# Probability products by whole quads, with the side jobs placed anew

## The chip, the cores and the metric

The kernel runs on one core of a Trainium2 chip. A core has five engines that run at once and meet only at semaphores: TensorE (PE, matmuls; its weight loads are shown as PEld), VectorE (DVE), ScalarE (ACT), GpSimd (POOL), and SyncE (SP), which here only issues DMAs. Matmul results go to PSUM, which has eight banks of 128 x 512 f32; all eight are in use. The metric is the time of one execution in microseconds (us), lower is better.

## The reference

Eight rows of 512 tokens and 256 features go through a cross attention with 16 heads of size 16, and then a linear two-layer network with its own weights for each row. All is f32.

```python
x = x + xattn(layernorm(x), ctx, ctx)          # per row b of 8:
#   q = (ln(x) @ Wq.T + bq) / 4 ; k = ctx @ Wk.T + bk ; v = ctx @ Wv.T + bv
#   attn = softmax(q k^T) for 16 heads ; y = x + (attn v) @ Wo.T + bo
h1 = einsum('gmh,goh->gmo', ln(y)[g], W1[g]) + b1[g]
h2 = einsum('gmo,gho->gmh', h1, W2[g]) + b2[g]  # no activation between
out = y + h2
```

Since nothing stands between the two layers, the kernel forms W1 and W2's product (w21) for each row and applies that.

## The kernel before

**Units.** The 16 heads of a row are four quads of four heads, and a quad has 16 units: four heads by four blocks of 128 keys. A row thus has 64 units, u = 0 to 63, and the program of every engine is one loop over rows (a turn) with an inner, unrolled loop over u. In a unit TensorE computes `st`, transposed scores of one head and key block (128 keys x 512 queries) of row b, and `nat`, the same scores the other way round (queries on partitions), 28 units ahead (LEAD), partly of row b+1. The two use different halves of the array's rows (64 x 128 tiles) and overlap. VectorE takes the row maximum of each `nat` (`neg_max`, L1036), ScalarE the exponential of each `st` into `probs` (L860). The maxima go into `st` as an additional row of the operand `qs`, so those of a quad must be there before its first `st`: they are turned by two small matmuls (`maxT`, L534, one for each half of the rows), copied to `max_hi` by VectorE (L1042), and carried to `qs` by a DMA (`store_max`, L367).

**Buffers.** `st` has 2 PSUM banks: `st` of unit u waits for the exponential of u-2. `nat` has 3, used as a ring, in which the turned maxima take a place too: a `nat` waits for the row maximum three places back.

**Probability products.** `pv(b, n)` (L547) multiplies the four exponentials of heads of one key block with V, in four 128 x 32 column tiles; four such calls, n = 4g to 4g+3, make a quad in the one bank `pv`. Before, two calls are made at u = 2, 10, 18, ... (L754), in what is called a bunch below, so a quad takes two bunches. Its result is copied out by ScalarE (`even_quad`, `odd_quad`), the sums of exponentials go through a DMA to `sums`, a reciprocal (`invert`, L1097) and two more DMAs (`save_inverse`, `spread_inverse`), and GpSimd multiplies (`divide`, L1305).

**Jobs.** Everything else of a row is cut into pieces, and tables give the unit after whose st and nat TensorE does each piece: XT (transposed normalised x, row b+1), K and Q (projections, row b+1, 12 pieces each), WO (output projection of row b-1, 8), V (row b+1, 8), YT (transposed normalised y, row b-1), Z (times w21, row b-1, 8), W21 (row b, 18, of which numbers 0 and 9 are the short ones of b2). All jobs share the two banks misc0 and misc1, so a job waits until the one before it has been copied out: K's result is copied by ScalarE and VectorE (`qk_move`) before Q may start, WO's is added to y and its statistics taken by VectorE (`y_half`, L1099, at the unit of WO's last piece and the next) before V may start, Z's is added to y (`out_half`, L1108) before W21 may start. `out_half` also waits for GpSimd's `add_b2`.

**Order.** Each engine works strictly in its written order; a wait holds up all that stands behind it. SP issues all DMAs of a turn in the order of its `turn` (L404), and GpSimd its work in that of L1340. The tables (L69 to L87) name units; EVEN, MASK, ODD, PAIR, INVERT, Y_NORM, CTX, X_STATS, X_NORM say where ScalarE and VectorE do their parts.

In the first turn there is no row before, so no WO, YT and Z; in the last none after, so no XT, K, Q and V, and no nat past u = 35.

## Time and profile before

| | |
|---|---|
| three runs, median (lowest to highest) | 552.11 us (547.64 to 553.07) |
| the profiled execution | 547.8 us, its span 545.9 us |
| mean granted TensorE clock | 0.994 |
| busy in the span: PE, DVE, ACT, POOL | 95%, 78%, 70%, 51% |

Times of rows are counted from the start of the span. A timeline row gives start, duration, engine, line, operation and tile; x8 means eight instructions merged, and one f32 matmul is two records. Durations of matmuls overlap, since they are pipelined, so what one costs is read from the distance of starts. What stands in brackets is the idle time ahead of it and what ended it.

### The profile page before, as it was taken

To read this page: it belongs to the slowest core of one execution; us is meant where nothing else is said; L and a number is where in the kernel's file an instruction comes from. 1 tells how busy PE (TensorE), PEld (TensorE's weight loads), DVE (VectorE), ACT (ScalarE), POOL (GpSimd) and SP (SyncE) were. 2 spreads that over 40 slices of the span, in tenths; PEclk is the share of its full clock that TensorE was granted. 3 is DMA by queue.
4 is the path that set the end of the run, shared out by engine and by line. 5 is a ranking of instruction groups with operands and counts; after the bars stand their busy time and mean duration, and the time that the engine had idled before them with its cause. 6 is when DMAs were issued, how large, how long until landed. Compare 5 with 4: busy or idle time off the path is not lost.

```text
span 545.9 us, 13272 instructions
## 1 busy us (share of the span) xinstructions
PE 521.2 (95%) x4229; PEld 328.9 (60%) x4229; DVE 425.7 (78%) x805; ACT 383.7 (70%) x707; POOL 276.3 (51%) x314
## 2 busy tenths in 40 slices
PE   8889999999999999999999999999999999899997
PEld 5555545675656665666666666567556766355556
DVE  4898887988887987888978988889878987785114
ACT  5437778767876768768786778768787776767732
POOL 3854606647356636648366454648276460309121
PEclk9989999999999999999999999999999999998999
DMA  6771245542454245450565235461554225340301
GB/s 209 184 249 76 61 112 144 161 135 60 135 161 177 60 111 168 141 166 21 134 168 201 59 68 150 139 201 26 116 152 178 64 61 146 74 173 2 99 0 39
DMA packets 34367, 65.29 MB, mean 120 GB/s; under 512 B 9810, under 2 KB 11930, under 8 KB 32282
## 3 DMA queue, kind: packets, MB, share of 16 engines
q1 hardware_dynamic: 34330, 64.81, 41.0%
q8 instruction: 21, 0.34, 0.3%
q14 instruction: 16, 0.13, 0.1%
HBM read 34.65 MB, written 4.44 MB: 72 GB/s over the span
## 4 chain that ended last, share of the span: by engine, by line
PE 67%; POOL 14%; DVE 9%; issue 4%; ACT 3%; DMA 1%; SPq 0%; POOLq 0%; DVEq 0%; ACTq 0%
PE pv L558 16%; PE st L544 12%; PE misc L671 10%; PE nat L527 8%; PE misc L630 8%; PE misc L643 6%; POOL b_part L1334 5%; DVE neg_max L1036 5%; POOL b_part L1329 4%; POOL y L1322 3%; ACT probs L860 2%; DVE y L1102 2%; DVE stats L1047 1%; POOL rstd L1264 1%; PE nat L583 1%
## 5 line engine op out<-in xcount | busy, mean ns | idle before, releaser
L1036 DVE TENSOR_REDUCE neg_max<-nat 128x1 f32<-128x512 f32 x512 | 329.4, 679 | 65.2 <-PE nat L527 64.1
L860 ACT ACTIVATE probs<-st 128x512 f32<-128x512 f32 x505 | 289.4, 598 | 113.0 <-PE st L544 102.3
L527 PE MATMUL nat<-ks,qs 63*128 63x512 f32 x512 | 237.1, 486 | 3.9 <-DMA qs<-lo 2.1
L544 PE MATMUL st<-qs,ks 64*128 64x512 f32 x505 | 231.0, 480 | 5.7 <-ACT probs L860 4.4
L544 PEld LDWEIGHTS st<-qs,ks 64*128 64x128 f32 x505 | 91.1, 186 | 75.3 <-ACT probs L860 44.4
L558 PE MATMUL pv<-probs,vs 128*32 128x512 f32 x1024 | 124.9, 605 | 0.0
L527 PEld LDWEIGHTS nat<-ks,qs 63*128 63x128 f32 x512 | 92.2, 185 | 19.5 <-DVE neg_max L1036 12.2
L671 PE MATMUL misc<-w_in 64*128 64x256 f32 x512 | 73.6, 378 | 0.0
L1261 POOL TENSOR_SCALAR var_eps<-mean_var 128x4 f32<-128x4 f32 x14 | 3.2, 227 | 119.5 <-DVE mean_var L1053 119.4
L558 PEld LDWEIGHTS pv<-probs,vs 128*32 128x32 f32 x1024 | 26.8, 109 | 56.6 <-issue 47.2
L671 PEld LDWEIGHTS misc<-w_in 64*128 64x128 f32 x512 | 50.6, 187 | 6.5 <-issue 0.8
L1315 POOL TENSOR_TENSOR y<-y,bo_all 128x256 f32<-128x256 f32 x32 | 22.4, 734 | 32.6 <-DMA y<-x 32.6
L1289 POOL TENSOR_TENSOR lo<-raw,hi 128x512 fp32r<-128x512 f32 x28 | 36.0, 1284 | 2.2
L1334 POOL TENSOR_TENSOR b_part<-b_part 128x1024 f32<-128x1024 f32 (+2 forms) x24 | 35.0, 1460 | 1.9
L1305 POOL TENSOR_TENSOR attnT<-pair_ctx,inv_sum 128x512 f32<-128x512 f32 x15 | 19.3, 1284 | 26.0 <-DMA inv_sum<-inv_dram 26.0
L643 PE MATMUL misc<-w,yT_in 64*128 64x256 f32 x224 | 31.0, 387 | 0.8 <-DVE yT_in L1069 0.2
L1287 POOL CAST hi<-raw 128x512 fp32r<-128x512 f32 x28 | 17.1, 611 | 28.6 <-DVE raw L1074 28.5
L643 PE MATMUL misc<-wo_in,attnT 64*128 64x256 f32 x224 | 31.3, 380 | 0.0
L1329 POOL TENSOR_TENSOR b_part<-w_in,b_in 128x2048 f32<-128x2048 f32 x8 | 28.8, 3603 | 0.0
L643 PEld LDWEIGHTS misc<-w,yT_in 64*128 64x128 f32 x224 | 22.2, 187 | 4.2 <-DVE yT_in L1069 3.0
L643 PEld LDWEIGHTS misc<-wo_in,attnT 64*128 64x128 f32 x224 | 22.4, 187 | 2.1
L1322 POOL TENSOR_TENSOR y<-y,b_all 128x256 f32<-128x256 f32 x28 | 19.5, 721 | 0.0
(155 smaller groups left out, 671.8 us busy)
## 6 DMA issues: line engine op xcount, KB each, us to landing
ks<-hi SPq DMA_DIRECT2D x64, 128.0 KB, 2.4
qs<-hi SPq DMA_DIRECT2D x64, 128.0 KB, 2.5
w_in<-w SPq DMA_DIRECT2D x8, 1024.0 KB
w_in<-w2T SPq DMA_DIRECT2D x8, 1024.0 KB
ctx_in<-ctxT SPq DMA_DIRECT2D x8, 512.0 KB, 4.7
ks<-lo SPq DMA_DIRECT2D x32, 128.0 KB, 2.4
qs<-lo SPq DMA_DIRECT2D x32, 128.0 KB, 2.5
y<-x SPq DMA_DIRECT2D x8, 512.0 KB, 3.4
```

Of the source, the lines that this page charges most:

```text
L527: mm(ring(at)[:, :], qs[rows, 2 * g + jj, c * P:(c + 1) * P], ks[rows, 2 * g + jj, :], start=True, stop=True).then_inc(nat_done, 1)
L544: mm(st_of(u, prep)[:, :], ks[rows, 2 * g + jj, kc * P:(kc + 1) * P], qs[rows, 2 * g + jj, :], start=True, stop=True).then_inc(st_done, 1)
L558: last = mm(pv_bank[32 * j:32 * j + 32, :], vs[:, kc, 4 * g + j, :], probs[n % 4][:, j, :], start=(kc == 0), stop=(kc == 3), tile_position ...
L630: last = mm(misc[m][:, :], (w_hi, w_lo)[left][rows, w, f, m * P:(m + 1) * P], src[right][rows, f, :], start=(i == 0), stop=(i == 11))
L643: last = mm(misc[half][:, s * D:(s + 1) * D], lefts[left][rows, f, c * P:(c + 1) * P], rights[right](rows, f), start=(i == 0 and n == 0), ...
L671: last = mm(misc[f][:, 0:D], w1_in[rows, o, f * P:(f + 1) * P], w2_in[rows, o, :], start=(phase == 0 and o == 0 and not b2), stop=(i == 2 ...
L860: act.activation(probs[kc % 4][:, j, :], st_of(u, prep)[:, :], ACT.Exp).then_inc(exp_done, 1)
L1036: dve.tensor_reduce(neg_max[:, g % 2, col:col + 1], ring(at_nat(n) if at is None else at)[:, :], AX.X, ALU.max, negate=True).then_inc(max_ ...
L1289: pool.tensor_tensor(lo[:, which, m, :], raw[:, which, m, :], hi[:, which, m, :].bitcast(F32), ALU.subtract).then_inc(lo_ready, 1)
L1322: last = pool.tensor_tensor(y[:, c, :], y[:, c, :], b2_all[:, :], ALU.add)
L1329: pool.tensor_tensor(b2_part[:, :, :], w2_in[:, :, :], b1_in[:, :].unsqueeze(2).to_broadcast([P, OC, D]), ALU.mult).then_inc(b2_step, 1)
L1334: pool.tensor_tensor(b2_part[:, 0:width, :], b2_part[:, 0:width, :], b2_part[:, width:2 * width, :], ALU.add).then_inc(b2_step, 1)
```

## The change

Two pv bunches of a quad become one bunch of four calls at u = 2, 18, 34, 50. `probs` grows from 16 to 19 tiles in a ring, so that three exponentials of the next quad can be written while a quad is still read. The maxima are turned one ring place later: the first half behind the unit's nat, the second behind its jobs, where they stood on both sides of st and nat. Nearly all tables change: K ends at 8 and Q begins at 10, WO ends at 25 and V begins at 28, Z ends at 49, and all of W21 is at 51 to 62. X's statistics go from 50 to 17, the copy of Q's other half from VectorE to ScalarE, the invert from 7 to 6, and the order of SP and GpSimd is changed.

```diff
-TURN_AFTER = 2
+AHEAD = 3
+TURN_AFTER = 3
-K_AT = (3, 4, 4, 4, 5, 5, 6, 7, 7, 8, 8, 9)
-Q_AT = (12, 12, 12, 12, 13, 13, 14, 15, 15, 16, 16, 16)
+K_AT = (3, 4, 4, 4, 5, 5, 6, 6, 7, 7, 8, 8)
+Q_AT = (10, 11, 12, 12, 12, 13, 14, 14, 15, 16, 16, 17)
...
-W21_AT = (44, 45, 46, 47, 48, 48, 52, 52, 54, 55, 56, 56, 57, 59, 60, 60, 61, 62)
+W21_AT = (51, 51, 52, 53, 54, 54, 55, 55, 56, 57, 57, 58, 58, 59, 60, 61, 61, 62)
...
+LAST_PV_AT = (56, 59, 62)
...
-        probs = [sb(f"probs{i}", [P, 4, S]) for i in range(4)]
+        probs = sb("probs", [P, 16 + AHEAD, S])
...
+        def prob_at(u):
+            g, i = u // 16, u % 16
+            return 16 - AHEAD + AHEAD * (g % 2) + i if i < AHEAD else i - AHEAD
...
                     turned = maxT_of(b, u, prep)
-                    if turned:
-                        maxT(*turned, TILES[1], prep).then_inc(maxT_half, 1)
                     st(b, u, prep)
                     for row, n in nats_of(b, u, post, prep):
                         nat(row, n)
                     if turned:
+                        maxT(*turned, TILES[1], prep).then_inc(maxT_half, 1)
+                    if u % 16 == 2:
+                        for n in range(4):
+                            if u > 16:
+                                pv(b, u // 16 * 4 - 4 + n)
+                            elif post:
+                                pv(b - 1, 12 + n)
+                    if not prep and u in LAST_PV_AT:
+                        pv(b, 12 + LAST_PV_AT.index(u))
+                    jobs(b, u, post, prep)
+                    if turned:
                         wait_apart(pe, maxT_half, 4 * turned[0] + turned[1])
                         maxT(*turned, TILES[0], prep).then_inc(maxT_done, 1)
-                    if u % 8 == 2:
-                        for n in (u // 4 - 2, u // 4 - 1):
...
-                if j == 0:
-                    wait(act, pv_done, 16 * b + kc - 3)
-                act.activation(probs[kc % 4][:, j, :], st_of(u, prep)[:, :], ACT.Exp).then_inc(exp_done, 1)
+                if u % 16 == AHEAD:
+                    wait(act, pv_done, 16 * b + u // 16 * 4)
+                act.activation(probs[:, prob_at(u), :], st_of(u, prep)[:, :], ACT.Exp).then_inc(exp_done, 1)
```

TensorE from the end of K to the start of Q (K's rows read ctx, Q's normedT), second turn, before:

```order
L630 MATMUL misc<-ctx_lo,w_hi 128x512 x2
L314 REGISTER_ALU
L544 MATMUL st<-qs,ks 128x512
L314 REGISTER_ALU
L527 MATMUL nat<-ks,qs 128x512
L558 MATMUL pv<-probs,vs 32x512 x8
...
L527 MATMUL nat<-ks,qs 128x512
L314 REGISTER_ALU
L630 MATMUL misc<-normedT_hi,w_hi 128x512 x2
```

and in the change:

```order
L638 MATMUL misc<-ctx_lo,w_hi 128x512 x2
L322 REGISTER_ALU
L552 MATMUL st<-qs,ks 128x512
L322 REGISTER_ALU
L535 MATMUL nat<-ks,qs 128x512
...
L535 MATMUL nat<-ks,qs 128x512
L322 REGISTER_ALU
L638 MATMUL misc<-normedT_hi,w_hi 128x512 x2
```

Between the two jobs stood three pairs of st and nat and a bunch; now two pairs stand there alone.

TensorE from the end of WO (it reads attnT) to the start of V (it reads ctx_hi with w_hi), same turn, before:

```order
L643 MATMUL misc<-wo_in,attnT 128x256 x4
L314 REGISTER_ALU
L544 MATMUL st<-qs,ks 128x512
...
L527 MATMUL nat<-ks,qs 128x512
L314 REGISTER_ALU
L558 MATMUL pv<-probs,vs 32x512 x8
...
L527 MATMUL nat<-ks,qs 128x512
L643 MATMUL misc<-w_hi,ctx_hi 128x256 x2
```

and in the change:

```order
L651 MATMUL misc<-wo_in,attnT 128x256 x4
L322 REGISTER_ALU
L552 MATMUL st<-qs,ks 128x512
...
L552 MATMUL st<-qs,ks 128x512
L322 REGISTER_ALU
L535 MATMUL nat<-ks,qs 128x512
L651 MATMUL misc<-w_hi,ctx_hi 128x256 x2
```

Three pairs stand in between in both, and the bunch has gone.

SP's DMAs from the gather of the sums to the spreading of their inverses (the load of ctx stood ahead of all this), now:

```order
L392 DMA sums<-even_sum 64x1x32
L393 DMA sums<-odd_sum 64x1x32
...
L350 DMA ctx_in<-ctxT 128x2x512
L322 REGISTER_ALU
L347 DMA x_in<-x 128x1024
...
L378 DMA qs<-max_hi 2x8x128
L322 REGISTER_ALU
L400 DMA inv_dram<-inv_small 4x16x32 x2
L322 ISA
L408 DMA inv_sum<-inv_dram 128x1x512
```

Here 1 MB of loads (ctx and x, 512 KB each) now stands directly ahead of the maxima and the inverses; only x stood there before, and the inverses were ahead of the maxima.

## Rows read from the trace of the kernel before

**Rows 1.** The page: busy time of each engine, share of the span, instructions.

```profile
PE 521.2 (95%) x4229; PEld 328.9 (60%) x4229; DVE 425.7 (78%) x805; ACT 383.7 (70%) x707; POOL 276.3 (51%) x314
```

**Rows 2.** Windows (length, busy by engine, clock, DMA share, GB/s): two whole turns.

```profile
280.59:343.50 62.91, 61.27 (x532) 39.44 (x536) 52.67 (x99) 47.02 (x89) 35.38 (x41) 1.00 0.43 127
466.86:528.54 61.68, 58.61 (x400) 30.33 (x404) 28.70 (x55) 40.80 (x77) 20.17 (x22) 0.97 0.22 71
```

**Rows 3.** Windows: one middle turn, from the bunch at u = 2, 18, 34, 50.

```profile
217.65:232.30 14.65, 14.65 (x116) 9.17 (x114) 12.61 (x22) 10.68 (x20) 9.08 (x11) 1.00 0.53 151
232.30:247.89 15.59, 15.46 (x147) 10.69 (x146) 13.38 (x29) 10.24 (x20) 7.25 (x10) 1.00 0.45 138
247.89:264.62 16.73, 15.89 (x143) 10.26 (x146) 14.05 (x24) 12.92 (x24) 10.12 (x9) 1.00 0.25 56
264.62:280.59 15.97, 15.32 (x134) 9.32 (x138) 12.72 (x27) 13.25 (x28) 8.53 (x13) 1.00 0.58 169
```

**Rows 4.** Timeline of PE around a bunch of two calls.

```profile
231.55 0.39 PE L544 MATMUL st<-qs,ks 64*128 64x512 f32 x1
...
231.81 0.49 PE L544 MATMUL st<-qs,ks 64*128 64x512 f32 x1
...
232.30 1.92 PE L558 MATMUL pv<-probs,vs 128*32 128x512 f32 x16
234.16 0.50 PE L544 MATMUL st<-qs,ks 64*128 64x512 f32 x1
...
234.50 0.39 PE L544 MATMUL st<-qs,ks 64*128 64x512 f32 x1
```

**Rows 5.** The chain that ended last (start, length, what): a single call.

```profile
528.54 0.99 PE pv L558 x8
```

**Rows 6.** Timeline of PE: two units with one W21 piece each.

```profile
262.03 0.58 PE L544 MATMUL st<-qs,ks 64*128 64x512 f32 x1
...
262.69 0.57 PE L544 MATMUL st<-qs,ks 64*128 64x512 f32 x1
```

**Rows 7.** Timeline of PE: the last matmuls of K.

```profile
224.41 0.43 PE L630 MATMUL misc<-ctx_lo,w_hi 64*128 64x512 f32 x2
```

**Rows 8.** Timeline of DVE: K's copy, and six reductions in a row.

```profile
225.53 0.73 DVE L1074 TENSOR_SCALAR raw<-misc,bqk 128x512 f32<-128x512 f32 x1
...
244.23 3.64 DVE L1036 TENSOR_REDUCE neg_max<-nat 128x1 f32<-128x512 f32 x6
```

**Rows 9.** Timeline of PE: last row of WO, first of V.

```profile
239.47 0.38 PE L643 MATMUL misc<-wo_in,attnT 64*128 64x256 f32 x1
...
242.70 0.39 PE L643 MATMUL misc<-w_hi,ctx_hi 64*128 64x256 f32 x2
```

**Rows 10.** Timeline of DVE: the two halves of WO's result.

```profile
239.89 0.69 DVE L1102 TENSOR_TENSOR y<-misc,y 128x512 f32<-128x512 f32 x1
...
241.97 0.68 DVE L1102 TENSOR_TENSOR y<-misc,y 128x512 f32<-128x512 f32 x1
```

**Rows 11.** Waits of DVE from 200.4 to 263.3 (us in total, times, longest).

```profile
DVE y L1111 <- POOL y L1322: 1.0, 1, 1.0
```

**Rows 12.** Timeline of SP's queue and of POOL: sums, inverses, divide.

```profile
221.28 0.56 SPq L385 DMA_DIRECT2D sums<-odd_sum  x1
...
224.69 1.14 SPq L392 DMA_DIRECT2D inv_dram<-inv_small  x2
...
227.21 0.62 SPq L400 DMA_DIRECT2D inv_sum<-inv_dram  x1
...
231.61 1.28 POOL L1305 TENSOR_TENSOR attnT<-pair_ctx,inv_sum 128x512 f32<-128x512 f32 x1 [1.09 <-DMA inv_sum<-inv_dram]
```

**Rows 13.** Windows: before and in a stretch with a lower clock, first turn.

```profile
32.60:38.00 5.40, 4.33 (x32) 2.50 (x30) 5.40 (x10) 2.78 (x5) 1.49 (x3) 1.00 0.93 277
38.00:41.40 3.40, 3.40 (x19) 3.13 (x16) 2.43 (x4) 1.19 (x2) 2.63 (x3) 0.50 0.98 391
```

**Rows 14.** The page, DMA issues: KB each, median us from issue to landing.

```profile
ctx_in<-ctxT SPq DMA_DIRECT2D x8, 512.0 KB, 4.7
```

105 lines of the change are left out of this document (49 added, 56 removed).

## The prediction

> **What bounds the kernel now.** I read the page first, then windows over whole turns and over the four quarters of a turn, then the timelines of TensorE and VectorE inside a turn, and last the waits. The page shows PE busy for 95% of the span, and DVE for 78% [rows 1]. The 95% overstates PE, since matmuls overlap in the records. A middle turn takes 62.9 us, of which DVE works 52.7 and ACT 47.0 [rows 2]; DVE has no more than 10 us of air in 63. PE and DVE are tied by a ring of three nat banks, so the slower of the two sets the pace of each short stretch: PE where jobs or bunches stand, DVE where units are bare. A bare pair of st and nat costs PE 0.26 us (231.55 to 231.81) [rows 4], a reduction costs DVE 0.61 (3.64 for six) [rows 8]. I take the turn in four quarters from bunch to bunch, which I call A (u = 2 to 18), B (18 to 34), C (34 to 50) and D (50 to 2): 14.65, 15.59, 16.73 and 15.97 us [rows 3], in sum 62.94.
>
> **What a bunch costs.** The pair ahead of it starts at 231.81 and the bunch at 232.30, so 0.49 where a pair takes 0.26: 0.23 to get in. From the bunch to the next pair it is 1.86 (232.30 to 234.16), and that pair takes 0.34 (to 234.50), 0.08 more than a pair [rows 4]. Two calls are 1.85 long [rows 4], one alone is 0.99 [rows 5], so a call more adds 0.86 and 0.13 is fixed. Entrance, fixed part and exit: 0.23 + 0.13 + 0.08 = 0.44, and up to 0.5 with the first weights. A bunch of four is 1.85 + 2 x 0.86 = 3.57. Four bunches fewer in a turn save 4 x 0.5 = 2.0 us, if PE is what everybody waits for at that place. This is the gain of the change, and it is sure only where nothing was hidden under the bunch.
>
> **What hid under the bunches that go.** Two of the four stood between two jobs on the same PSUM banks.
>
> K to Q (the bunch at u = 10, quarter A). K's last matmul starts at 224.41 [rows 7]; VectorE finishes its copy at 225.53 + 0.73 = 226.26 [rows 8], 1.85 later, since reductions stand ahead of it. Under the bunch nobody saw this. Now K ends at u = 8, Q starts at u = 10, and TensorE has only the rest of K (0.23) and two pairs (0.5) to do. It will stand at Q's first matmul for 1.85 - 0.73 = 1.1 us. Taking the pair copy out of the way (u = 3 to 12) makes VectorE's backlog 0.6 shorter at best, the earlier invert makes it 0.3 longer: 0.5 to 1.5, and I take 1.1. Behind the waiting matmul stand the next st and nat, so ACT and DVE run empty too. A then is 14.65, less the bunch at 10 (2.35 with its switch), plus two calls more in the bunch at 2 (1.71), plus 1.1, less 0.2 for the maxima (below): 14.9.
>
> WO to V (the bunch at u = 26, quarter B). WO's last matmul starts at 239.47, V's first at 242.70 [rows 9]: 3.2 us, set by VectorE, which adds the first half at 239.89, takes its statistics, does a reduction, and ends the second add at 241.97 + 0.68 = 242.65 [rows 10]. The bunch and three pairs filled all of that but 0.4. The change leaves three pairs, 0.8 us, so TensorE will stand for some 2.4 us ahead of V, with the nat banks full. V starts no sooner for the bunch having gone; its work is added at u = 18 instead. B is 15.59 + 1.71 (longer bunch) + 0.26 (one more pair ahead of WO's end) - 0.6 (V is done one unit sooner) - 0.2 = 16.8. If the wait were 1 us shorter, B were 15.8.
>
> C: the bunch at 42 goes (-2.35), that at 34 grows (+1.71), five W21 pieces and a short one move to D. A piece costs 0.66 (262.03 to 262.69) less a pair [rows 6], 0.42, the short one about half, in sum -2.35. The wait of `out_half` for GpSimd's `add_b2`, 1.0 us [rows 11], which held W21's start, should go too: `add_b2` now comes ahead of `b2_parts`, and Z ends under the long bunch at 50. Units 37 to 39 are bare now, and DVE's 0.61 sets their pace instead of PE's 0.26: 3 x 0.35, some 0.9. C is 16.73 - 2.35 + 1.71 - 2.35 - 1.0 - 0.2 + 0.9 = 13.4.
>
> D: the bunch at 58 goes, that at 50 grows, W21's pieces arrive: 15.97 - 2.35 + 1.71 + 2.35 - 0.3 = 17.4. The copy of W21 at u = 62 ahead of the next XT is as it was.
>
> **The turned maxima.** Now the first half no longer holds up st and nat, and the second is behind the jobs, so its wait for the first is filled. Nothing shows this price alone. Below it is nothing (DVE is late and the ring waits one place later anyway), above it is a pair and a half, 0.4, for each of four. I take 0.2 to 0.3.
>
> **Costs that I set at nothing.** The statistics of x (1.8 us of VectorE) go from the bunch at 50 to that at 18, which is 3.57 long and covers them with two reductions (1.2). Q's second copy on ScalarE falls under the same bunch. y's normalisation (2.1 us of ScalarE) falls under that at 34. Without that cover each would cost its own length once in a turn. The ring of 19 lets ScalarE go on for three units, but only two st banks feed it, so in a bunch of 3.57 it does two exponentials as before; this ring saves nothing by itself, it only makes the long bunch harmless.
>
> **Sum.** A 14.9 + B 16.8 + C 13.4 + D 17.4 = 62.5, against 62.94: 0.4 less, and times six turns 2.5 us. In the first turn the gain and the wait at Q nearly cancel, and W21 moves out of bare units, where it was free, into full ones: +1. The last turn, 61.68 long [rows 2], has no V and few jobs, so it is paced by ACT and DVE; it loses the cover of y's halves in B but is shorter in C: 0, give or take 3. From the profiled execution, 547.8, the sum is 547.8 - 2.5 + 1 = 546.3. A further low-clock stretch in the now longer runs of bare units (35 to 49 in the first turn, 3 to 17 in the last) would add 1.7, as 3.4 us at clock 0.50 cost [rows 13], and I count one: 548. The median of the runs shown, 552.1, is 4.3 above the profiled time; I put the forecast 1 above the sum on that account, 549.
>
> **Rivals.**
> Faster: the waits at Q and V come out small, because VectorE, which idles in each long bunch, arrives without backlog. For it speaks that DVE has 10 us of air in a turn [rows 2]. Against it speaks that both waits are chains of VectorE's own work behind PE's last matmul, 1.85 and 3.2 us long, and air elsewhere doesn't shorten them. Without either, DVE's work would bound A (14.1) and B (15.2): 0.8 + 1.6 = 2.4 us less in a turn, six turns, 14.4: 533 to 535. With half of it 541. Point of decision: waits below half of 1.1 and 2.4. Chance 0.31.
>
> Slower, by SP's order: the maxima and inverses, 8 KB each, now stand behind 1 MB of loads. Before, from the issue of the second sums at 221.28 to the end of GpSimd's division at 231.61 + 1.28 it took 11.6 us [rows 12]. That issue is 3.6 us behind the start of the bunch at 2 (217.65) [rows 3], and now 1.7 more: at 5.3, so the division ends at 16.9, and WO comes at 14.9 + 3.57 + 0.9 = 19.4, 2.5 us of slack. 512 KB of ctx take 4.7 us to land [rows 14]; I estimate both loads at 6 to 7, which is until 12.7. The inverses were on DRAM by 227.21, 5.9 behind the sums [rows 12], which would be 11.2 now: if they wait for the loads they are 1.5 late, and the slack shrinks to 1. The maxima would come at 12.7 too, and st of u = 16 wants them at some 13. If each small transfer loses 1 us more, either use is 1 to 2 us late, six times: 555 to 560. That is 0.14. The Trainium skill, DMA: Bandwidth & Descriptors, section on queues, rings and completion order, says that descriptors are consumed in ring order on each DMA engine, which would make small transfers of the same queue wait so; no row here shows a small one caught behind a large one.
>
> Slower, by the clock: in the first turn a stall of some 2 us after thin units was followed by 3.4 us at clock 0.50, which is 1.2 GHz of 2.4 [rows 13]. If the stall ahead of V does the same in each turn, V runs at half the clock and a turn gains 1.7 us: six times 1.7 is 10, 558. Against it: WO stands densely ahead of that stall, and the before kernel's stall ahead of XT never cost a clock in the middle turns (1.00) [rows 2]. Chance 0.13. The Trainium skill, TensorE: Matmul & The Clock Gate, Part 1, says the clock falls after the array has been idle and comes back with activity; by this rule a longer wait in every turn is a danger, and it speaks against this change.
>
> **How the numbers follow.** Forecast, within 1% (a measurement of this kernel can tell about 1%, 5.5 us, from no change): 0.42. Faster 0.31, slower 0.14 + 0.13 = 0.27. The range reaches from the half case of the faster rival with 3 us to spare, 538, to the clock rival with 2, 560; about 1 in 10 is left out at each end. The likeliest case's own range is 543 to 555 (quarters off by 0.5 us each way in six turns, first and last turn by 3).
>
> **What would show it.** In the profile after: bunches of 32 records 3.6 us long at u = 2, 18, 34, 50, four a turn. TensorE standing about 1.1 us ahead of the first Q matmul and 2.4 ahead of V's first, put down to VectorE. No wait of VectorE for GpSimd at `out_half`. Quarters near 14.9, 16.8, 13.4, 17.4 and a turn near 62.5. ACT's wait for st should be fewer and longer. I am wrong if V starts under 2.5 us behind WO's last matmul, if C doesn't shrink by 3 us, if PE waits for a DMA at u = 16 or 20, or if the clock falls in middle turns.

## The result and the profile after

The changed kernel takes 572.8 us in the median of its runs (569.9 to 576.4), the kernel before 552.6 beside it: a ratio of 1.040, 95% interval 1.035 to 1.046. That is slower by 4%, outside the range, on the side that had 0.27. The profiled execution has a span of 574.6 us, 28.7 more than before's 545.9. That is more than the 20.2 us between the medians: after's profiled execution is the slowest of its four (576.4 us, clock 0.950), before's is one of its fastest (547.8 us, clock 0.994), while other executions of before at 551.6 to 553.5 us have a mean clock of 0.978 to 0.984. The accounts below are of the two profiled executions.

In kernel.py of after, st is L552, nat L535, pv L566, K and Q L638, WO and V L651, the reductions L1044, the adds of WO's result L1110. The page of after, engines' busy time and the granted clock in 40 slices, beside [rows 1]:

```profile
PE 538.1 (94%) x4229; PEld 347.8 (61%) x4229; DVE 425.9 (74%) x798; ACT 386.1 (67%) x714; POOL 277.0 (48%) x314
PEclk9889879899999899998999899998999899887999
```

VectorE and ScalarE do the same work as before and idle more; the instructions of PE are the same in number. The clock's row is what is new: an 8 in nearly every turn. Its mean over the span is 0.950, before 0.994. At half clock for the rest, that is 0.050 x 2 x 574.6 = 57 us at 1.2 GHz against 7.

Windows of after over the quarters A, B, C and D of a middle turn, beside [rows 3] (length, busy by engine, clock, DMA share, GB/s):

```profile
230.46:245.50 15.04, 14.57 (x120) 9.34 (x118) 11.88 (x21) 10.37 (x20) 10.84 (x14) 1.00 0.62 183
245.50:263.88 18.38, 16.91 (x150) 11.95 (x148) 15.76 (x37) 11.17 (x20) 8.13 (x12) 0.91 0.41 118
263.88:277.94 14.06, 13.73 (x116) 8.64 (x112) 12.03 (x21) 11.89 (x23) 10.38 (x10) 1.00 0.34 111
277.94:295.26 17.32, 16.70 (x159) 12.11 (x156) 13.05 (x23) 13.75 (x28) 5.97 (x6) 1.00 0.30 88
```

The turn is 64.80 us instead of 62.94: A +0.4, B +2.8, C -2.7, D +1.35. B is the only quarter at a clock below 1.00. TensorE there, from WO's last matmul to V, beside [rows 9]:

```profile
254.88 0.38 PE L651 MATMUL misc<-wo_in,attnT 64*128 64x256 f32 x1
...
256.26 0.49 PE L535 MATMUL nat<-ks,qs 63*128 63x512 f32 x1
258.11 0.38 PE L651 MATMUL misc<-w_hi,ctx_hi 64*128 64x256 f32 x2 [1.35 <-DVE y L1110]
...
259.14 0.41 PE L651 MATMUL misc<-w_hi,ctx_hi 64*128 64x256 f32 x2
259.36 0.41 PE L651 MATMUL misc<-w_hi,ctx_lo 64*128 64x256 f32 x2
```

V starts 3.23 us behind WO's last matmul, to the hundredth what it was before (239.47 to 242.70); TensorE stands for 1.35 of them; the three pairs in between filled the rest, up to 256.26 + 0.49. Then V's rows come about 0.21 us apart. In a kernel below whose clock holds they are 0.12 apart. Waits of TensorE over the whole span (us in total, times, longest):

```profile
PE misc L651 <- DVE y L1110: 8.2, 6, 1.4
...
PE misc L638 <- POOL normedT_lo L1285: 4.8, 4, 2.0
```

The last of these is a wait of Q's first matmul, and 2.0 of it are in turn 1 (the second), as will be seen.

Spans of all turns, from the st of u = 2 to that of the next turn, us, by the windows of the traces. `early_y` and `fixed` are experiments told below:

| turn | 0 | 1 | 2 | 3 | 4 | 5 | 6 | 7 |
|---|---|---|---|---|---|---|---|---|
| before | 58.2 | 61.1 | 62.9 | 62.9 | 62.9 | 62.8 | 60.6 | 60.6 |
| after | 62.4 | 66.5 | 65.1 | 64.8 | 64.7 | 64.9 | 64.0 | 66.9 |
| early_y | 62.5 | 62.4 | 64.7 | 64.7 | 64.8 | 64.5 | 62.2 | 66.6 |
| fixed | 64.6 | 62.4 | 63.5 | 63.4 | 63.4 | 63.3 | 62.2 | 66.0 |

Of the 28.7 us, 1.5 are ahead of turn 0 (a low-clock stretch at 19.4), 8.1 in turns 2 to 5, 5.3 in turn 1, 3.4 in turn 6, and 10.5 in the first and last turn together. The stretch ahead of turn 0 comes and goes with the execution rather than with the change: `singles` and `best3` below, which begin as before does, have one at 19.6 and 17.7, and `early_y`, which begins as after does, has none.

### The profile page after: what moved, and what is told of

Read it like the earlier page. It is cut to its first block, busy times and chain, and to the rows that moved or that the text cites. A ratio compares the mean times of both kernels' runs of the same rounds, so it can differ in the third digit from the quotient of the medians.

```text
span 574.6 us, 13174 instructions
## 1 busy us (share of the span) xinstructions
PE 538.1 (94%) x4229; PEld 347.8 (61%) x4229; DVE 425.9 (74%) x798; ACT 386.1 (67%) x714; POOL 277.0 (48%) x314
## 4 chain that ended last, share of the span: by engine, by line
PE 66%; issue 11%; POOL 9%; DVE 7%; DMA 3%; ACT 3%; SPq 1%; DVEq 0%; POOLq 0%; ACTq 0%
PE pv L566 17%; PE misc L651 13%; PE st L552 11%; PE nat L535 8%; PE misc L638 5%; PE misc L679 5%; DVE neg_max L1044 4%; POOL normedT_lo L1285 2%; POOL y L1321 2%; ACT probs L867 2%; DVE y L1110 2%; POOL b_part L1340 2%; DMA inv_sum<-inv_dram 1%; POOL b_part L1335 1%; PE nat L591 1%
## 5 line engine op out<-in xcount | busy, mean ns | idle before, releaser
L1044 DVE TENSOR_REDUCE neg_max<-nat 128x1 f32<-128x512 f32 x512 | 332.9, 683 | 98.1 <-PE nat L535 95.6
L535 PE MATMUL nat<-ks,qs 63*128 63x512 f32 x512 | 256.9, 514 | 4.6 <-DVE neg_max L1044 2.2
L552 PE MATMUL st<-qs,ks 64*128 64x512 f32 x505 | 252.5, 510 | 6.3 <-ACT probs L867 4.2
L552 PEld LDWEIGHTS st<-qs,ks 64*128 64x128 f32 x505 | 97.6, 195 | 71.2 <-ACT probs L867 40.8
L566 PE MATMUL pv<-probs,vs 128*32 128x512 f32 x1024 | 122.0, 616 | 0.0
L535 PEld LDWEIGHTS nat<-ks,qs 63*128 63x128 f32 x512 | 98.8, 196 | 16.8 <-DVE neg_max L1044 10.6
L566 PEld LDWEIGHTS pv<-probs,vs 128*32 128x32 f32 x1024 | 30.4, 113 | 70.1 <-issue 58.5
L651 PE MATMUL misc<-w,yT_in 64*128 64x256 f32 x224 | 37.8, 379 | 0.0
L651 PE MATMUL misc<-wo_in,attnT 64*128 64x256 f32 x224 | 33.0, 379 | 0.0
L1302 POOL COPY vs<-v_nat 128x256 f32<-128x256 f32 x32 | 12.6, 398 | 35.4 <-DVE v_nat L1088 21.7
L651 PE MATMUL misc<-w_hi,ctx_hi 64*128 64x256 f32 x112 | 20.6, 357 | 8.2 <-DVE y L1110 8.2
L651 PEld LDWEIGHTS misc<-w,yT_in 64*128 64x128 f32 x224 | 27.0, 186 | 0.8 <-PE misc L651 0.2
L651 PEld LDWEIGHTS misc<-wo_in,attnT 64*128 64x128 f32 x224 | 23.3, 186 | 2.5
```

What stands on the lines that cost most here:

```text
L535: mm(ring(at)[:, :], qs[rows, 2 * g + jj, c * P:(c + 1) * P], ks[rows, 2 * g + jj, :], start=True, stop=True).then_inc(nat_done, 1)
L552: mm(st_of(u, prep)[:, :], ks[rows, 2 * g + jj, kc * P:(kc + 1) * P], qs[rows, 2 * g + jj, :], start=True, stop=True).then_inc(st_done, 1)
L566: last = mm(pv_bank[32 * j:32 * j + 32, :], vs[:, kc, 4 * g + j, :], probs[:, prob_at(4 * n + j), :], start=(kc == 0), stop=(kc == 3), til ...
L651: last = mm(misc[half][:, s * D:(s + 1) * D], lefts[left][rows, f, c * P:(c + 1) * P], rights[right](rows, f), start=(i == 0 and n == 0), ...
L1044: dve.tensor_reduce(neg_max[:, g % 2, col:col + 1], ring(at_nat(n) if at is None else at)[:, :], AX.X, ALU.max, negate=True).then_inc(max_ ...
```

## The experiments

Ratios are against the kernel before on the same chip, with 95% intervals. Quarters are of turn 3 unless another is named.

### The bunches by themselves

**bunch_only**: before, with one bunch of a quad, the ring of 19 and the last turn's three single calls (`LAST_PV_AT`), all tables of jobs and orders as they were.

```diff
-                    if u % 8 == 2:
-                        for n in (u // 4 - 2, u // 4 - 1):
+                    if u % 16 == 2:
+                        for n in range(4):
```

> The kernel before, with only the bunch changed: whole quads at u = 2, 18, 34, 50 and the ring of 19 tiles, every table, the maxima and the orders of SP and GpSimd as before. Theory 1 (bunches covered waits between jobs): four switches of 0.5 are saved in a turn, but the covers at u = 10 (K to Q), 26 (WO to V) and 42 (Z to W21) are gone; with V's stall of 2.3, Q's of 0.9, W21's wait for out_half of 1 to 2 us more, and a low clock behind the stall, a middle turn is 64 to 66 us and the whole 565 to 580. Theory 2 (the new tables and orders are at fault, the bunch is the gain): a middle turn is about 61, the whole 535 to 542.

Measured: 585.4 us, 1.066 (1.058 to 1.074), the slowest of the plain edits; theory 1, with the turn 0.7 and the whole 5 us above its ranges. Its quarters:

```profile
229.53:244.89 15.36, 14.79 (x123) 9.66 (x118) 12.41 (x22) 10.63 (x20) 9.13 (x10) 1.00 0.44 131
244.89:262.11 17.22, 15.37 (x148) 10.85 (x148) 13.37 (x28) 10.39 (x19) 7.45 (x10) 1.00 0.47 149
262.11:279.45 17.34, 16.14 (x142) 10.51 (x140) 14.30 (x24) 13.02 (x24) 10.62 (x9) 1.00 0.22 49
279.45:296.22 16.77, 15.11 (x134) 9.36 (x131) 12.45 (x27) 12.65 (x27) 7.66 (x12) 1.00 0.53 150
```

And the waits that its timeline of TensorE names in that turn, start first, wait and releaser in brackets (a sixth, 0.61 ahead of XT, is in before's turn as well, with 0.60):

```profile
240.33 0.50 PE L551 MATMUL st<-qs,ks 64*128 64x512 f32 x1 [0.49 <-ACT probs L866]
...
255.44 0.50 PE L551 MATMUL st<-qs,ks 64*128 64x512 f32 x1 [0.41 <-ACT probs L866]
257.42 0.39 PE L650 MATMUL misc<-w_hi,ctx_hi 64*128 64x256 f32 x2 [1.40 <-DVE y L1108]
...
275.78 0.49 PE L675 MATMUL misc<-b_part,ones 64*128 64x128 f32 x4 [0.93 <-DVE y L1117]
...
292.21 0.50 PE L551 MATMUL st<-qs,ks 64*128 64x512 f32 x1 [0.99 <-ACT probs L866]
```

The turn is 66.7 us with the clock at 1.00 throughout, 3.8 more than before, though it holds four switches fewer. TensorE's busy time is the same (14.79 + 15.37 + 16.14 + 15.11 = 61.4, before 61.3), so what is added is standing: the five waits are 4.2 us, of which before's turn has 0.74, at W21. A bunch that goes from between two jobs uncovers the wait for the copy of the first job's result (V's 1.40), and st runs into ScalarE three times, in A, B and D. That is 3.5 of the 3.8.

V waits 1.39 to 1.40 us in each of turns 1 to 6 of this kernel, but the clock falls only in 1, 2 and 5. B of turn 2, with the fall, to be read beside B of turn 3 above:

```profile
178.56:197.07 18.51, 16.66 (x150) 11.82 (x146) 14.13 (x29) 10.47 (x19) 9.02 (x10) 0.91 0.36 107
```

18.5 instead of 17.2, in one and the same execution: a stretch of 3.4 us at 0.50 costs 1.3.

**singles**: before, each bunch of two calls as two single ones, one unit apart; eight switches more in a turn.

```diff
-                    if u % 8 == 2:
-                        for n in (u // 4 - 2, u // 4 - 1):
+                    if u % 8 in (1, 2):
+                        n = u // 4 - 2 if u % 8 == 1 else u // 4 - 1
```

> The kernel before with each bunch of two calls parted into two bunches of one, a pair of st and nat between them (u = 1 and 2, 9 and 10, ...): the price of a switch by itself, with every wait between jobs covered as before. The prediction's price of 0.44 to 0.5 us gives eight switches a turn, 3.5 to 4 us: middle turn 66.4 to 66.9, the whole 549 + 7.5 x 4 = 576 to 580. If a switch costs nothing where TensorE is not the slowest (rival), under 65 and under 568.

Measured: 568.3 us, 1.033 (1.028 to 1.038). The turn is 65.1 us, 2.2 more for eight switches, 0.28 each:

```profile
229.55:244.53 14.98, 14.98 (x121) 9.12 (x117) 13.15 (x22) 11.42 (x20) 8.93 (x10) 1.00 0.51 154
244.53:260.31 15.78, 15.59 (x150) 10.23 (x147) 13.50 (x29) 10.39 (x20) 7.48 (x10) 1.00 0.39 117
260.31:277.13 16.82, 16.40 (x142) 9.71 (x139) 13.96 (x23) 12.61 (x23) 9.49 (x9) 1.00 0.28 63
277.13:294.69 17.56, 16.26 (x135) 9.06 (x132) 12.48 (x26) 12.95 (x26) 9.19 (x13) 1.00 0.54 156
```

The two of D cost 0.8 each, those of A and B 0.1 to 0.2, and C's nothing (16.82 against 16.73). The time is just outside the rival (under 568 us, under 65), and far from the 576 to 580 by the prediction's price. In C TensorE has a wait to give away, 0.74 us at W21 in before's turn, and none of 0.35 or more is left there with the single calls. A has no such wait either before or here, and its switches are cheap all the same; why D's are not was not tested.

**split_ab** and **split**: after, with two calls at u = 10, 18, 26, 34 in quads 0 and 1 (split_ab), or in all quads as before (split). The copies out of the bank that this needs are moved too (`PAIR_AT`, in split `ODD_AT` as well), and split ends the last turn as before does, without the three single calls.

```diff
-                    if u % 16 == 2:
-                        for n in range(4):
+                    if u in (10, 18, 26, 34):
+                        for n in (u // 4 - 2, u // 4 - 1):
+                            pv(b, n)
```

> The changed kernel with the bunches of quads 0 and 1 split in two calls each again (u = 10, 18, 26, 34) and VectorE's pair copy of the row before at u = 3 again, which the bunch at 10 needs; quads 2 and 3 stay whole and all tables else are the new ones. Theory 1 (the removed bunches had covered the waits K to Q and WO to V): two switches come back at 0.5 us each, but the wait of about 0.9 ahead of Q goes, the stall of 1.7 ahead of V falls under 0.5, and the clock no longer falls in the middle turns: a middle turn goes from 64.8 to about 62.5 to 63, and the whole to 556 to 561. Theory 2 (the waits are due to where VectorE and the SP queue put the work, not to the missing bunches): the turn grows by the two switches to 65.8, the whole to 579.

> The changed kernel with all four bunches split in two (u = 2, 10, 18, 26, ...) as in the kernel before, and the pair copies at u = 39 and 3 again; all jobs, the maxima and the orders of SP and GpSimd are the new ones. Against the kernel with only quads 0 and 1 split (555.7, middle turn 62.5) two more switches come back in a turn. Theory 1 (C and D hid no wait of their own in the bunches that went, so there the switch is a plain cost): middle turn 63.3 to 63.6, but the first and last turn lose their low-clock stretches: the whole 555 to 559. Theory 2 (every split helps, a switch costs next to nothing): middle turn under 62.5, the whole under 552.

Measured: split_ab 555.7 us, 1.012 (1.004 to 1.020); split 563.7, 1.026 (1.021 to 1.031). split_ab's quarters A and B are 16.49 and 15.32, in sum 31.8 against 33.4 of after, at a clock of 1.00, and C is 13.41: theory 1. split has 14.74, 15.35, 15.45 and 18.24: splitting quads 2 and 3 too costs 3.0 us in C and D and gives back 1.7 in A; the turn is at theory 1's bound, the whole 5 us above its range. The long bunches pay in C and D; in A and B, where K and Q, WO and V need the cover, they don't. split_ab is the best that was got out of the changed kernel, and it is not under before.

**maxima**: before, with the change's turned maxima alone.

```diff
-                    if turned:
-                        maxT(*turned, TILES[1], prep).then_inc(maxT_half, 1)
                     st(b, u, prep)
...
+                        maxT(*turned, TILES[1], prep).then_inc(maxT_half, 1)
...
                     jobs(b, u, post, prep)
+                    if turned:
+                        wait_apart(pe, maxT_half, 4 * turned[0] + turned[1])
+                        maxT(*turned, TILES[0], prep).then_inc(maxT_done, 1)
```

> The kernel before with one part of the change alone: both turned maxima on the other side, the first behind the unit's nat, the second behind its jobs, one ring place later. Theory 1 (the prediction's term): each quad saves 0.2 to 0.3 us, 1 us a turn, so a middle turn of 61.9 us instead of 62.9 and some 541 to 545 us in all, ratio 0.985 to 0.99. Theory 2: the maxima cost nothing where they stood, because the ring's wait for the row maximum comes right behind them at either place; middle turn 62.8 to 63.0, ratio 0.997 to 1.003. Theory 3: the later place delays the first nat behind it: over 63.3 us a turn, ratio above 1.01.

Measured: 549.2 us, 0.998 (0.995 to 1.002). Quarters 14.81, 15.50, 16.80, 15.79: 0.2 more in A, 0.1 to 0.2 less in B and D, the turn 62.90. Theory 2; in the kernel before, the place of the maxima is worth nothing.

### The clock behind WO

**warm_v**: after, with filler matmuls on the whole array at u = 26, 27 and 28, ahead of V, into the pv bank, once ScalarE has copied it out; their products are used nowhere. **warm_tile** is the same on 64 rows of the array.

```diff
+                        fill(6 if u == 28 else 1, 7)
...
+                    mm(misc[bank][:, 0:P], ident[:, :], ones[:, :], start=True, stop=True)
```

In warm_tile the operands are `ident[TILES[0], :]` and `ones[TILES[0], :]`.

> The changed kernel with eight small matmuls added, whose result is read by nobody, in each turn that has both WO and V: one at u = 26, one at 27, six at 28, ahead of V's first matmul, where TensorE stands idle. Theory 1 (the stall ahead of V takes TensorE's clock down to half, and V then runs at half): the clock stays at 1.0 in the middle turns, V's pieces start 0.12 us apart again, quarter B falls from 18.4 to about 17.1 us and a middle turn from 64.8 to 63.5; over six turns 8 us less, about 565. Theory 2 (the fall of the clock is a by-product and VectorE sets the pace there anyway): quarter B stays at 18.4 or grows by what the added matmuls take, the time stays at 573 or rises by 1 to 3. In both the wait for VectorE's second add ahead of V stays, 8.2 us in all in the changed kernel, only filled.

> The changed kernel with the filler matmuls of warm_v (1, 1 and 6 of them at u = 26, 27 and 28, into the bank of the probability products), but on 64 of the array's rows, as the work around them is tiled, instead of all 128. Their products are used nowhere. Theory 1 (a filler on the whole array drains the units around it, and that took back what the clock gave): no low clock in the middle turns as in warm_v, and quarter B at 16.7 to 17.0 us instead of 17.5; 562 to 566 us, ratio about 1.025. Theory 2 (the fillers' own columns cost it): B stays at 17.4 to 17.6 and the time at 569 to 571 us. Theory 3: fillers of half the array do not hold the clock: B about 18.4 and low clock in each turn, about 573 us.

Measured: warm_v 570.8 us, 1.040 (1.032 to 1.049), as slow as after; warm_tile 566.9, 1.029 (1.022 to 1.036). Quarter B of warm_v:

```profile
239.97:257.46 17.49, 17.49 (x165) 12.48 (x164) 15.46 (x37) 11.25 (x20) 7.49 (x11) 1.00 0.39 117
```

and of warm_tile:

```profile
239.64:256.70 17.06, 16.96 (x164) 12.93 (x164) 15.14 (x36) 11.09 (x20) 7.11 (x11) 1.00 0.37 104
```

And warm_tile's timeline of TensorE at the start of V, to be read beside after's:

```profile
252.24 0.39 PE L656 MATMUL misc<-w_hi,ctx_hi 64*128 64x256 f32 x2
252.46 0.28 PE L656 MATMUL misc<-w_hi,ctx_lo 64*128 64x256 f32 x2
252.58 0.28 PE L656 MATMUL misc<-w_lo,ctx_hi 64*128 64x256 f32 x2
```

V's rows are 0.12 us apart now. Both hold the clock at 1.00 where after has 0.91, and B falls from 18.38 by 0.9 and 1.3. The 1.3 is the price of one low-clock stretch in V, with nothing else changed but the standing filled. The fillers on the whole array give 0.43 of it back. In warm_v the second add of WO's result is done at 252.52 (251.84 + 0.68) and V starts at 253.12, 0.60 later, since the fillers are still running; in warm_tile it is 252.18 and 252.24. warm_v's whole time shows no gain; one reason is that A came out at 16.2 us in turn 4, where Q waits 1.59 for GpSimd (the load of y, below). In whole times warm_tile ended near its theory 1 (562 to 566), warm_v did not (565).

**adds_first**: after, with both adds of WO's result (`y_add`) at u = 25 and all statistics a unit later.

```diff
-                statistics(1, b, y, 2 * half, 2 * half + 2)
...
+                if half == 0:
+                    y_add(b)
+                    return
+                wait(dve, y_ready, 2 * b + 2)
+                statistics(1, b, y, 0, 4)
```

> The changed kernel, but VectorE does both adds of WO's result to y at once at u = 25 and the statistics of both halves at 26, so that V may start 1.4 us sooner (a statistics pair of 0.75 and a reduction of 0.6 no longer stand ahead of the second add). Theory 1: the wait of TensorE for the add falls from 1.35 to near 0 in each turn, the clock may stay up; quarter B goes from 18.4 to 16 to 17, the whole to 560 to 565. Theory 2 (VectorE's total work in B sets its length, wherever V starts): B falls by less than 0.5 us, the whole stays within 3 us of 573.

Measured: 567.2 us, 1.034 (1.026 to 1.043). B is 16.69 at a clock of 1.00, the middle turn 63.1: what released V came sooner, and the clock never fell there. The whole is 2 us above theory 1's range. The run names VectorE's chain (add, statistics, reduction, add) as the cause of the standing, and the standing as what went ahead of the fall.

In the middle turns of warm_v, warm_tile and adds_first, without that standing, the clock falls nowhere in B. But the standing doesn't always bring the fall: besides the three turns of bunch_only, early_y (below) has V's wait in turns 1 and 6 with no fall. Its row in turn 1:

```profile
124.36 0.39 PE L651 MATMUL misc<-w_hi,ctx_hi 64*128 64x256 f32 x2 [1.38 <-DVE y L1110]
```

And in split_ab, split and best the clock falls in turn 4, 2 to 3 us behind a wait of 0.8 ahead of YT that stands in all their middle turns (in split once more, in turn 6, behind 0.7). So the length of the wait alone doesn't decide it; what else does is open.

**warm_all**: warm_v, and one whole-array filler in each bare unit of the first and last turn (its core):

```diff
+                    if not post and 35 <= u < 50:
+                        fill(1, 0)
+                    if not prep and 3 <= u < 18:
+                        fill(1, 0)
+                    if not prep and 26 <= u < 34:
+                        fill(1, 7)
```

> The changed kernel with the eight added matmuls ahead of V in the middle turns, and one small added matmul (0.2 us, read by nobody) in each bare unit of the first turn (u = 22 to 27, 35 to 49) and of the last (3 to 17, 26 to 33). Theory 1 (thin stretches cost clock, and the low clock falls on the long bunches that follow): hardly a low window is left beside the one in the prologue, the first turn goes from 62.4 to about 60, the last from 66.9 to about 64, the middle turns are those of the kernel with the added matmuls ahead of V alone (63.7); in all 4 to 6 us under that kernel (570.8), so 565. Theory 2 (the first and the last turn are long for want of cover): both stay within 1 us of 62.4 and 66.5, the whole at 570.

Measured: 573.4 us, 1.042 (1.036 to 1.047). Neither theory foresaw that. The mean clock rose to 0.985, the last turn's A is 16.82 at 1.00 against 13.90 at 0.80: the fillers cost 2.9 more than the clock they kept. Bare units are paced by VectorE and ScalarE, so a half clock is cheap in them, and filling is not. What a half clock does cost there is the next bunch. After's timeline, TensorE: the bunch at u = 34 of turn 3, and that at u = 18 of the last turn, behind bare units:

```profile
263.88 0.40 PE L552 MATMUL st<-qs,ks 64*128 64x512 f32 x1
264.20 3.64 PE L566 MATMUL pv<-probs,vs 128*32 128x512 f32 x32
267.78 0.50 PE L552 MATMUL st<-qs,ks 64*128 64x512 f32 x1
...
503.51 5.61 PE L566 MATMUL pv<-probs,vs 128*32 128x512 f32 x32
509.05 0.49 PE L552 MATMUL st<-qs,ks 64*128 64x512 f32 x1
```

5.61 us for 3.64; the clock is 0.50 up to 507.5, for 4.0 us of it. The same happens to the bunches at u = 50 of the first turn and u = 34 of the last, where the steps from pair to pair are 6.1 and 5.4 us, for 3.9.

### The load of y

**early_y**: after, with SP's load of x into y ahead of the maxima, the inverse and a quad's K and Q, and GpSimd's add_bo ahead of the division.

```diff
                 save_inverse(b, 0)
+                load_y(b)
...
                 spread_inverse(b, 0)
...
-                load_y(b)
```

> The changed kernel with one thing moved: SP issues the load of x into y before the maxima, the inverse and K's and Q's quad, instead of behind them, and GpSimd adds bo ahead of the division. Theory 1 (GpSimd reaches normedT_lo late, since it waits for that load, and Q's first piece waits for normedT_lo): turn 1's quarter A falls from 17.4 to about 15.2 us, the middle turns' A from 15.0 to 14.3 to 14.6, the whole by 4 to 6 us, ratio about 1.03. Theory 2 (Q's wait is that for VectorE's copy of K, GpSimd only comes close to it): A stays at 15.0 in the middle turns, and turn 1 alone gains 2 us. Theory 3: the load ahead of the inverse delays WO, and B grows by what A gains.

Measured: 568.1 us, 1.029 (1.023 to 1.035). Timeline of after in turn 1, POOL first:

```profile
103.39 2.85 POOL L1321 TENSOR_TENSOR y<-y,bo_all 128x256 f32<-128x256 f32 x4 [4.77 <-DMA y<-x]
...
108.79 1.27 POOL L1285 TENSOR_TENSOR normedT_lo<-xT_raw,normedT_hi 128x512 fp32r<-128x512 f32 x1
```

Then TensorE, Q's first matmul:

```profile
110.20 0.50 PE L638 MATMUL misc<-normedT_hi,w_hi 64*128 64x512 f32 x2 [1.96 <-POOL normedT_lo L1285]
```

Windows of turn 1, A and B, of after:

```profile
98.86:116.30 17.44, 15.48 (x121) 10.25 (x118) 12.59 (x22) 10.53 (x20) 11.77 (x14) 0.90 0.52 157
116.30:134.30 18.00, 16.43 (x148) 11.40 (x148) 15.18 (x36) 11.20 (x20) 7.14 (x12) 0.91 0.46 147
```

and of early_y:

```profile
97.49:111.98 14.49, 14.20 (x121) 8.92 (x117) 11.73 (x21) 10.34 (x19) 9.41 (x11) 1.00 0.58 168
111.98:128.80 16.82, 15.25 (x149) 10.43 (x148) 15.24 (x36) 11.21 (x20) 7.34 (x11) 1.00 0.42 123
```

SP issues the load late; GpSimd, which works in its written order, stands at add_bo, splits XT late, and Q's first matmul waits 2 us for it. Turn 1 gains 4.1 us, 3.0 in A and 1.2 in B, and both of its low-clock stretches are gone; turn 6 gains 1.8. The whole gains 4.8 us, as theory 1 had it, but in middle turns A stays at 15.03: there Q waits for VectorE's copy (theory 2), and the load is only close behind. Of B's 1.2 the moved load is not shown to be the cause, since V waits in turn 1 as long as before the move (1.38). Nor does the wait for GpSimd belong to turn 1: warm_tile, where the load is late as in after, has none of 0.35 or more in turn 1, but 1.62, 1.71 and 2.19 in turns 3, 5 and 6, and adds_first has 1.43 in turn 5. In early_y and fixed it is nowhere.

**fixed**: early_y and warm_tile together; no other edit.

> The changed kernel with the edits of warm_tile and of early_y together. Theory 1 (two separate causes, so the gains add): quarter B 17.05 us as in warm_tile, A 15.0 in every middle turn as in early_y, middle turn 63.2 to 63.5, turn 1 at 62, in all 559 to 562 us, ratio about 1.017. Theory 2 (one hides the other): A stays at 16 us as in warm_tile, the time at 565 to 567 us.

Measured: 563.6 us, 1.021 (1.016 to 1.025). A is 15.03, B 17.08, C 14.07, D 17.18, the quarters of theory 1; the whole is 1.6 above its range. The two gains add up within the intervals: 1.1% of before's time each alone, 2.0% together.

### W21 in twelve units

**wide**, **fixed_wide**, **wide2**: after, fixed, and fixed with the weights' load early, each with Z at u = 38 to 42 and W21 from 46 on, and GpSimd's parts of b2 moved for it.

```diff
-Z_AT = (40, 41, 42, 43, 45, 46, 47, 49)
-W21_AT = (51, 51, 52, 53, 54, 54, 55, 55, 56, 57, 57, 58, 58, 59, 60, 61, 61, 62)
+Z_AT = (38, 39, 39, 39, 40, 41, 41, 42)
+W21_AT = (46, 47, 48, 49, 49, 51, 52, 53, 54, 55, 56, 57, 57, 58, 59, 60, 61, 62)
...
+                    load_ffn(b)
                 store_max(b, 2)
```

The last lines are wide2's alone.

> The changed kernel with Z's pieces at u = 38 to 42 instead of 40 to 49 and W21's at 46 to 62 instead of 51 to 62; for this GpSimd makes b2's product ahead of the root of y's variance, add_b2 right behind the roots, and the sums of b2's parts last. Theory 1 (the packed W21 costs quarter D its 1.4 us, and the bare units ahead of it in the first and last turn lower the clock): D of middle turns 15.9 to 16.3 instead of 17.3, C 14.6 to 15.0 instead of 14.06, so 0.3 to 0.6 us less a turn; D of the first and last turn 17 and 18.5 us instead of 18.9 and 20.3; in all 565 to 569 us. Theory 2 (the work only moves from D to C): sum of C and D unchanged at 31.3 to 31.5 in middle turns, 571 to 574 us. Theory 3 (b2 comes late for the first of W21's pieces): a wait of TensorE for b_part at u = 46, and C above 15.5 us.

> The changed kernel with all the edits of fixed and of wide. Theory 1: as in wide, 0.3 to 0.6 us a turn and 3 us in the first and last turn less than fixed, 553 to 556 us. Theory 2: as fixed, 559 to 562 us. If it comes under the kernel before, the change's bunches are worth having once the jobs are placed well; at 553 or more they are not.

> fixed_wide with one more thing moved: SP issues the loads of w1, w2 and b ahead of the third quad's maxima and of quad 0's K and Q, as in the kernel before. Theory 1 (W21 packed into 12 units costs quarter D its length): no wait at b2's product, D of middle turns 15.6 us as in fixed_wide, C 14.8 to 15.3, so a middle turn of 62.6 to 63.1; first turn 60.5 us, last 64; in all 552 to 557 us against 563.6 of fixed. Theory 2 (the work only moves from D to C): middle turn 63.3 us and 559 to 563 us in all, less only by the 4 us of the first turn. Theory 3 (the 2 MB of loads now stand in front of the maxima): TensorE or VectorE waits for max_rows at u = 34, quarter B longer by more than 1 us.

Measured: wide 644.3 us, 1.167 (1.159 to 1.174); fixed_wide 633.7, 1.151 (1.143 to 1.159). Both missed all theories, and by an error of mine: in the changed order SP issues the load of w1 and w2 behind quad 2's maxima, and b2's product, put ahead of GpSimd's roots, waits for it with all that is behind, also the root that y's normalisation needs: TensorE stands 8 to 9 us ahead of YT in each of turns 1 to 5. A row of wide:

```profile
288.45 3.60 POOL L1335 TENSOR_TENSOR b_part<-w_in,b_in 128x2048 f32<-128x2048 f32 x1 [16.25 <-DMA b_in<-b]
```

wide2, with the load early: 571.4 us, 1.036 (1.029 to 1.043), slower than fixed and outside all three theories (C is 16.6 where 15.3 was the most). Its C and D:

```profile
258.09:274.69 16.60, 16.08 (x137) 10.63 (x134) 13.26 (x24) 12.40 (x24) 9.84 (x13) 1.00 0.27 73
274.69:290.31 15.62, 15.13 (x139) 10.35 (x136) 11.67 (x21) 13.17 (x28) 4.72 (x5) 1.00 0.26 71
```

D loses 1.56 us and C gains 2.53. C and D together are 31.3 in fixed, 32.2 here and 32.7 before, so the packing of W21 doesn't cost the middle turns anything. It pays only together with the long bunches: the packed tables with short bunches (split) take 33.7 in C and D, the long bunches with before's tables (bunch_only) 34.1. In the last turn it looks otherwise. Windows, C and D of after's last turn:

```profile
521.54:535.47 13.93, 13.63 (x101) 7.20 (x101) 4.39 (x8) 10.90 (x22) 10.23 (x8) 0.89 0.02 4
535.47:555.74 20.27, 20.27 (x151) 10.88 (x147) 1.29 (x2) 10.69 (x20) 5.30 (x7) 1.00 0.23 66
```

and of before's:

```profile
494.46:510.64 16.18, 15.78 (x121) 8.69 (x121) 5.87 (x11) 11.35 (x23) 10.68 (x9) 0.89 0.02 4
510.64:526.98 16.34, 16.22 (x113) 8.70 (x109) 0.00 (x0) 10.06 (x20) 4.06 (x5) 1.00 0.26 81
```

D + 3.9, C - 2.25: 1.7 us in sum. They are neither W21's place nor the three single calls at 56, 59 and 62. In before, D has five calls of pv (u = 50, 58 and 62), in after seven (50, 56, 59 and 62), while C has four in both: the two that before makes at u = 58 of turn 6 now stand at u = 2 of the last turn, and two calls cost 2 x 0.86. (The first turn has two fewer.) Two runs bear it out; both have W21 packed and nine calls in C and D, as before does, split without the single calls and split_ab with them:

```profile
508.18:521.53 13.35, 12.86 (x101) 6.85 (x101) 4.76 (x9) 10.82 (x22) 10.04 (x8) 1.00 0.03 9
521.53:539.77 18.24, 18.24 (x134) 10.50 (x131) 1.29 (x2) 10.58 (x20) 5.46 (x7) 1.00 0.20 70
...
502.05:513.37 11.32, 10.81 (x85) 6.37 (x85) 4.75 (x9) 10.81 (x22) 8.17 (x6) 1.00 0.02 4
513.37:533.64 20.27, 20.27 (x150) 10.84 (x147) 1.29 (x2) 10.69 (x20) 7.36 (x9) 1.00 0.21 66
```

The first two are split's, the others split_ab's; the sum is 31.59 in both, 0.9 under before's, whose C has the clock at 0.89. wide2's last turn is no better than after's (17.26 and 18.98, in sum 36.2).

### A version faster than both

**best** puts split_ab, adds_first and fillers into one. **b2_early** takes before and moves only GpSimd's work, **best3** adds adds_first to it, **best2** the turned maxima as well.

```diff
+                b2_begin(b)
                 if post:
                     inverse_root(1, b - 1)
-                b2_parts(b)
-                if post:
                     add_b2(b - 1)
+                b2_end(b)
```

`b2_begin` is the product, 3.6 us, and `b2_end` the sums.

> Quads 0 and 1 in two bunches of two, 2 and 3 whole (as in the kernel with those two split), both adds of WO's result first and the statistics behind, and one small added matmul in bare units of the first turn (20 to 25, 35 to 49) and the last (3 to 17, 28 to 33). Middle turn 62.5 less 0.3 for V's rest of a wait = 62.2, first turn 61.3 to 59.5, last 62.5 to 61.5: 555.7 - 2 - 2 - 1 = 550 or less, about what the kernel before takes (549). If the low windows of the first and last turn cost nothing, 554.

> The kernel before with the b2 edit of best2 alone: product ahead of the root of y's variance, add_b2 behind it, sums last. Theory 1 (it carries best2's gain): quarter C 16.1 us instead of 16.8, middle turn 62.1 to 62.3, 544 to 546 us, ratio 0.987 to 0.992; best2's other two edits bring the rest through quarter B. Theory 2 (the gain needs the adds of WO first too): middle turn 62.7 to 62.9, ratio within 0.5% of 1.

> The kernel before with b2_early's edit and both of WO's adds ahead of the statistics, without the turned maxima of best2. Theory 1 (the maxima cost 0.2 us in quarter A and give 0.1 in B, so they do nothing): A 14.6, B 15.1 to 15.2, C 16.1 to 16.4, middle turn 61.6 to 62.0, ratio 0.985 as best2's. Theory 2 (best2 needs the maxima): middle turn 62.2 or more, ratio about 0.993.

> The kernel before with three edits: the turned maxima as in the changed kernel; both of WO's adds to y ahead of the statistics; and on GpSimd the product of b2's parts ahead of the root of y's variance, add_b2 right behind that root and the sums of b2's parts last, so that the adds of Z (rows 11, 1.0 us) find b2 already added. Theory 1: the wait ahead of W21 (0.94 us of TensorE in each middle turn) goes: middle turn 61.5 to 62.0 us, 540 to 545 us in all, ratio 0.98 to 0.99, the first version faster than the kernel before. Theory 2: what VectorE gains there it loses in front of its row maxima, so the turn stays at 62.7 to 63.0 and the ratio within 1%. If the run maxima is also at 1.00, all of the gain is b2's.

Measured: best 558.4 us, 1.015 (1.010 to 1.020), no better than split_ab and above its forecast (550, or 554): its middle turn is 62.4, its last 66.6. b2_early 548.9, 0.998 (0.994 to 1.001); best3 545.2, 0.989 (0.987 to 0.992); best2 542.7, 0.986 (0.981 to 0.991), the fastest. best2 came out as its theory 1; the other two stand between their theories (turn 62.5 and 62.2 us), with b2_early's whole at theory 2. best2's quarters:

```profile
215.93:230.74 14.81, 14.81 (x121) 9.36 (x117) 12.51 (x22) 10.51 (x20) 9.52 (x11) 1.00 0.55 158
230.74:245.87 15.13, 15.13 (x148) 10.66 (x147) 13.38 (x28) 10.20 (x19) 9.85 (x10) 1.00 0.47 146
245.87:261.96 16.09, 15.78 (x142) 10.71 (x140) 14.41 (x24) 13.19 (x24) 7.86 (x8) 1.00 0.24 54
261.96:277.73 15.77, 15.05 (x134) 9.39 (x132) 12.33 (x27) 12.97 (x27) 8.06 (x13) 1.00 0.57 165
```

The 1.0 us of VectorE at `out_half` [rows 11] is gone in all three. Alone this takes 0.4 from C (16.37); with the adds first B falls by 0.4 more (15.63 to 15.25). Between best2 and best3 the turn differs by 0.4 (61.8 and 62.2) and the intervals overlap, so whether the maxima help there is open.

## Why the prediction was wrong

**The switch, 0.5 us: right at its place, wrong as a sum.** A bunch of four runs from the pair at 263.88 to the next at 267.78 in after, 3.90, so 3.64 without the pair; two of two were 2 x (2.35 - 0.26) = 4.18. That is 0.54 for one switch. But the step took four of them as 2.0 in the turn, "if PE is what everybody waits for at that place". By singles a switch is worth 0.28 in the mean, from 0.8 in D down to nothing in C, and the middle turn of bunch_only, with four fewer, is 3.8 us longer.

**K to Q and WO to V: the lengths right, the standing half of what was said.** V starts 3.23 us behind WO (2.5 was the bound), since VectorE's chain sets it, A is 15.04 (14.9), and B without the fall of the clock 17.06 (16.8). But TensorE stands 1.35 ahead of V for the 2.4 forecast, because the three pairs behind WO take 1.9 us (254.88 to 256.75) and not 0.8, and 0.47 ahead of Q in turn 3 for 1.1. Q's wait is thus below the half that was named as the point of decision, and the faster rival's gain did not come with it. A has 0.6 less wait than its sum and is still 0.1 longer; 0.2 of that is the maxima, the rest is not explained, so that A came out is in part luck.

**The clock: the step that failed.** The sum had one more low-clock stretch, 1.7 us; the case in which V runs at half the clock in each turn had 0.13. It happens in each of turns 1 to 6, which is 7.5 us by B of after less B of fixed (1.1 to 1.4 a turn); once more in turn 1 behind Q's wait, 1.0; and in the first and last turn behind bare units, where three bunches run at half clock, 2.2, 2.4 and 1.5 us, 6 in sum. With the 1.5 ahead of turn 0, which is not the change's, that is 16 of the 28.7 us. The reason given against it, that before's stall ahead of XT never cost a clock, was a comparison with a shorter one: the trace of before has 0.7 us at most for XT, V's is 1.35. But a stall as long as V's goes without a fall in three turns of bunch_only and two of early_y, so that it would come in every turn could not be known from its length. The mechanism stood in the prediction with its place and nearly its price (1.7 from [rows 13], where PE was paced by less; 1.3 in V). Even that rival ended at 558: it did not have the bunches of the outer turns. The Trainium skill, TensorE: Matmul & The Clock Gate, Part 1, says that the clock falls when the array idles; this speaks for that rival. The trace agrees in that adds_first and warm_tile, which shorten or fill the standing, keep 1.00 in B; the five turns just named show the same standing at 1.00.

**Maxima, 0.2 to 0.3 for each of four: wrong.** They are worth nothing (0.998): 0.2 too much in each of A, B and C, and up to 0.3 in D.

**C, 13.4 for 14.06.** The wait at `out_half` did go, but it was entered at its full 1.0 and b2_early has 0.4 for it: the 1.0 is VectorE's standing, TensorE's at that place is 0.74 in before, and of that more than half is gained. With the maxima's 0.2 that is 0.8, more than the whole miss. C shrank by 2.7 us, not by the 3 that the prediction had set as a sign of being wrong. D is 17.32 (17.4).

**SP's order: the rival as told didn't come, another one did.** (Before, the inverses were stored ahead of the maxima but spread behind them; now both stand behind.) No wait of TensorE for a DMA at u = 16 or 20. What came late was the load of y, which stands last in SP's new order and holds GpSimd, and by it Q: 2.0 us in turn 1, which with the clock behind it are 3.0 in A, and 0.3 to 0.7 in turns 2, 5 and 6. The prediction looked at the small transfers behind the large ones, and never at who waits for the last in the list.

**The first and last turn: +1 and 0 for +4.2 and +6.2.** A, B and C of after's last turn have a granted clock of 0.80, 0.77 and 0.89, before's 1.00, 1.00 and 0.89. The sum treated these turns as paced by others than TensorE, which holds in their bare units and not in their bunches, now twice as long; and D of the last turn, 20.27 for 16.34, has TensorE full, with two calls more, 1.7 us, which the sum didn't move from turn 6 into the last.

**In sum.** The middle turns without the clock are at +0.5 (fixed: 63.36 for 62.87) where -0.4 was forecast. Of the 0.9 missed the maxima and `out_half` explain all and more, 1.2 to 1.5; other terms erred the other way. In the profiled execution the clock is 16 us, the late load of y without its stretch of low clock 3.3, the turns' own growth 4.8 (0.5 in each of turns 2 to 5, 1.2 and 1.6 in turns 1 and 6, by fixed). What is left, 4 to 5 us, lies in the first and last turn and was not taken apart further.

## What to carry to other kernels

Merging short blocks of another kind saves the switch only where no one waits behind it; ask of each block that is taken away what wait it covered, and put another job there first. A new stall of TensorE must be priced twice: once as time, and once as the clock of the work behind it, as a bound for every turn and not once a run, since the same stall cost the clock in all six turns of one kernel, three of another and none of those that filled it. When an order of DMAs is rewritten, follow the transfer that has become last to whoever stands in order behind its user.

## What the runs showed of the hardware

- One stretch of 3.4 us at 1.2 GHz costs 1.3 us in V's work (bunch_only, B: 18.51 and 17.22); a bunch that is at half clock for 4.0 us takes 2.0 more (5.61 for 3.64); and in bare units a low clock costs less than a small filler in each of them (13.90 us at 0.80 against 16.82 at 1.00).
- Eight fillers of 128 columns on the whole array cost 0.43 us more than eight on 64 rows, among work tiled by 64 rows (17.49 and 17.06): the latter are over when V may start, the former hold it back by 0.6.
- The same wait of 1.35 to 1.40 us is followed by a fall of the clock in all of turns 1 to 6 of after, in three of bunch_only and in four of early_y.
- The same switch between 64 x 128 and 128 x 32 tiles costs 0.8 us, 0.2 or nothing, by the quarter in which it stands.
